# Gate weights made in the grouping stage, and scores scanned two blocks ahead at a block's end, in an eleven-stage graph network kernel

## The chip, the cores and the metric

The kernel runs on one core of a Trainium2 chip. The core has five engines with instruction streams of their own: TensorE (PE, with its weight loads as PEld), VectorE (DVE), ScalarE (ACT), GpSimd (POOL) and SyncE (SP). The metric is the device time of one execution in microseconds (us).

## The reference, cut to what matters

Four layers, each followed by a residual sum and a layer normalization over 256 columns: a rotation matrix made of 50,000 plane rotations, a relational graph attention network, a filter convolution over the edges, and a mean over the edges' sources. There are 3125 nodes and 50,000 edges sorted by destination. The change touches the second layer:

```
q_node = query[batch]                      # batch is all zeros: one query for all nodes
gh   = relu(concat([x, q_node]) @ gate_w1 + gate_b1)
gate = sigmoid(gh @ gate_w2 + gate_b2)
x0   = x * gate
h    = concat([x0, q_node, x * q_node])
h = relu(rgat(h, W1, q1, k1, b1))                  # 4 heads of 128
h = h + relu(rgat(h, W2, q2, k2, b2))              # 4 heads of 128
h = relu(rgat(h, W3, q3, k3, b3))                  # 1 head of 128

def rgat(x, W, Q, K, b):                           # 2 edge types
    xw    = einsum('ni,rio->rno', x, W)
    alpha = leaky_relu(xw[etype, dst] @ Q + xw[etype, src] @ K, 0.2)
    alpha = segment_softmax(alpha, dst)
    return segment_sum(xw[etype, src] * alpha, dst) + b
```

## The kernel before, in words

The program is a row of stages. Each has its own buffers and semaphores and ends with a barrier of all engines. The ones that matter, in order: the edge lists (`edge_order`), the grouping stage (`source_order`, buffers named bucket_), the gate stage (`nodes_gate`, gate_), then three times an attention (`attention`, sum_) and its projection (`nodes_attend`, attend_), the mixing, the filter convolution and the source mean.

Nodes stand in 25 tiles of 125. Edges are laid out in 432 steps of 125, no step crossing a node tile's border. Twelve steps are a block, so an attention has 36 blocks; a block has three parts of four steps.

The grouping stage counts the edges of each source tile and works out where each edge goes in a list by source. Nearly all of it is VectorE on arrays of 125 x 10,000; TensorE does five small products.

The gate stage takes the node tiles in seven groups of four (the last has one). Per group: `turn` multiplies by the rotation, `residual`, `statistics`, `root` (POOL), `scale` give x1; `turn_x1`, `gate_hidden`, `gate_outer`, `turn_x0` make the gate and x0; `table(t)` projects one tile on both edge types and `take(t)` adds the query's constant part and puts it in one of three output buffers (RING = 3). Before the first group it loads the gate's and projection's weights (`projection_load`), and makes the score weights (`score_weights`), the scaled weights and the query's constant rows; every engine waits for them (`ready`). SP stores a group's table rows only after x0 of the next group is made. POOL also scatters 150 edge columns (`group_edges`).

The attention's engines each run in program order:
- POOL gathers the 432 steps' rows into a ring of three blocks. A part of a slot is gathered again once the sums of the block three before it have used that part (line 1198).
- ACT scales the rows of a block by the softmax weights, 40 activations a block with four heads (`scale`), after the block's weights are made; behind a block's rows comes the exponential of the next block (`weights`).
- TensorE sums a part's four steps with `sums` into PSUM. After part 0 of block s it does `list_ends(s+1)`, after part 1 `turn_carry(s+1)`, after part 2 `turn_weights(s+1)` and `turn_scores(s+2)`.
- VectorE makes the selection matrices (`pick`), adds the sums (`add_part`), and makes the weights: `score` (needs the gathered rows of the block two ahead), `spread_in_tiles` (two scans along the edges, then `ends_made`), `spread_over_tiles`, `shift`, `grow`, `take_weights`.
- The weights of block s+1 are made while block s is summed. In block s VectorE does: load of six registers (`part_tiles`); spread_in_tiles(s+1); pick(1); add_part(0); spread_over_tiles(s+1); pick(2); add_part(1); shift(s+1); score(s+2); grow(s+1); add_part(2); take_weights(s+1); pick(s+1, 0).

Where the four steps of a part belong to one node tile, they are summed together and added once; else each is added by itself, VectorE first loads four registers (`node_tiles`), and TensorE waits for the adds. Of the 108 parts of an attention 16 are of that kind (L1466 has 120 instances in an attention, 72 + 3 x 16). VectorE's loop holds six blocks with four heads and three with one head, TensorE's and ACT's loops three.

## Time and profile before

| | us |
|---|---|
| median of 3 runs | 6628.7 (6625.0 to 6634.2) |
| the profiled execution | 6613.5 |
| its span | 6611.7 |
| gate stage, first load to the first load of the next stage | 1138 to 1586 |
| attention 1, 2, 3, first gather to last sum | 1592 to 2396, 2724 to 3530, 3763 to 4472 |

Over the span PE is busy 66%, DVE 48%, ACT 30%, POOL 54%. Times below are us from the span's start. In a row, what stands in brackets is how long the engine sat idle before the instruction and what ended that; "issue" is time in which it waited for nothing that the profile shows. Rows of a gather give POOL's time to issue it, not the transfer.

### The profile page before, as it was taken

Reading aid. Unit: us, or ns where it says so; the run is one execution under the profiler, and the core shown is the slowest. Engines: PE = TensorE matmul, PEld = TensorE weight load, DVE = VectorE, ACT = ScalarE, POOL = GpSimd, SP = SyncE. Lnnn points to the kernel's source line nnn. Section 1 sums busy time; section 2 is a strip of 40 time slices with the busy share of each in tenths; the row PEclk is TensorE's granted clock in tenths of the full one; section 3 lists DMA queues with packets and bytes.
Section 4 is the critical chain, followed back from the end, with each engine's and each line's share of the span. In section 5 each row is a group of like instructions: output and inputs, shape, how many; then the busy total and the mean of one; then the engine's idle time right before and its main releaser. Section 6 shows DMA issues by size and latency. Waiting matters only on the chain. (4 is left out here: it accounts for less than half of the span.)

```text
span 6611.7 us, 81270 instructions
## 1 busy us (share of the span) xinstructions
PE 4356.9 (66%) x17924; PEld 3140.3 (47%) x17925; DVE 3158.4 (48%) x7294; ACT 2007.4 (30%) x4713; POOL 3596.5 (54%) x2941
## 2 busy tenths in 40 slices
PE   5599720785776779676677544448788888765553
PEld 5588610443554555355556533334455555443332
DVE  6577556122554532354453244443466666433334
ACT  0122200001655520265552022211566666410000
POOL 0244410366776637776674788760355555238884
PEclk6799955797887879788786555555899999876565
DMA  0000011324665523566551233332333333233333
GB/s 7 24 10 11 10 31 42 91 62 107 168 163 138 150 72 74 127 167 157 137 151 42 46 85 84 85 77 75 80 93 94 94 94 93 67 86 84 84 84 73
DMA packets 515758, 565.41 MB, mean 86 GB/s; under 512 B 308626, under 2 KB 400639, under 8 KB 515225
## 3 DMA queue, kind: packets, MB, share of 16 engines
q0 software_dynamic: 359872, 381.65, 23.9%
q1 hardware_dynamic: 155606, 181.09, 9.7%
q14 instruction: 234, 1.92, 0.1%
q8 instruction: 46, 0.75, 0.1%
HBM read 467.37 MB, written 92.22 MB: 85 GB/s over the span
## 5 line engine op out<-in xcount | busy, mean ns | idle before, releaser
L1200 POOL DMA_INDIRECT sum_gx_sb<-scratch_xw,keep_k_row_step_sb x1296 | 1609.4, 1242 | 560.0 <-issue 361.5
L1313 PE MATMUL sum_a_ps<-sum_gx_sb,sum_sel_sb 125*125 125x258 f32 (+1 forms) x4320 | 1232.0, 450 | 554.3 <-ACT sum_gx_sb L1249 250.5
L1313 PEld LDWEIGHTS sum_a_ps<-sum_gx_sb,sum_sel_sb 125*125 125x125 f32 x4320 | 950.7, 246 | 750.6 <-issue 556.5
L1249 ACT ACTIVATE sum_gx_sb<-sum_gx_sb,sum_wt_sb 125x129 f32<-125x129 f32 x3312 | 981.7, 388 | 468.6 <-DVE sum_wt_sb L1441 468.6
L2377 POOL DMA_INDIRECT filter_gx_sb<-scratch_h,keep_k_src_step_sb x432 | 519.5, 1202 | 540.9 <-DVEq L2522 394.3
L2809 POOL DMA_INDIRECT source_gx_sb<-scratch_h,source_grouped_sb x432 | 533.6, 1235 | 155.9 <-issue 117.6
L2821 PE MATMUL source_s_ps<-source_gx_sb,source_sel_sb 125*125 125x257 f32 x864 | 376.9, 613 | 312.0 <-DMA source_gx_sb<-scratch_h,source_grouped_sb 312.0
L1107 POOL DMA_INDIRECT scratch_grouped<-keep_k_value_sb,keep_k_place_sb x400 | 476.2, 1191 | 123.7 <-issue 123.7
L2821 PEld LDWEIGHTS source_s_ps<-source_gx_sb,source_sel_sb 125*125 125x125 f32 x864 | 251.5, 305 | 437.2 <-issue 173.7
L2431 PE MATMUL filter_ps<-filter_m_sb,filter_h_sb 128*125 128x256 f32 x1760 | 407.1, 385 | 50.7 <-DVE filter_f_sb L2496 50.7
L2431 PEld LDWEIGHTS filter_ps<-filter_m_sb,filter_h_sb 128*125 128x125 f32 x1760 | 322.4, 188 | 180.5 <-issue 135.6
L2846 DVE TENSOR_TENSOR keep_agg_sb<-source_s_ps,keep_agg_sb 125x257 f32 x432 | 184.5, 427 | 391.8 <-PE source_s_ps L2821 383.7
L532 POOL TENSOR_TENSOR turn_lm_sb<-turn_lt_sb,turn_masks_sb 128x512 f32<-128x512 f32 x23 | 29.2, 1272 | 536.5 <-DVE turn_lt_sb L466 536.5
L1466 DVE TENSOR_TENSOR keep_agg_sb<-sum_a_ps,keep_agg_sb 125x516 f32 (+1 forms) x360 | 202.0, 561 | 234.8 <-PE sum_a_ps L1313 132.6
L1613 PE MATMUL attend_x_ps<-attend_w_sb,attend_ht_sb 128*125 128x512 f32 (+1 forms) x800 | 281.9, 526 | 37.3 <-ACT attend_ht_sb L2083 37.3
L2449 PE MATMUL filter_ps<-filter_ms_sb,filter_sel_sb 125*125 125x256 f32 x864 | 214.8, 392 | 135.3 <-DVEq L2521 135.3
L1242 ACT ACTIVATE sum_wexp_sb<-sum_dw_sb 48x126 f32<-48x126 f32 (+1 forms) x108 | 33.3, 308 | 719.2 <-DVEq L1431 719.2
L2492 DVE SCALAR_TENSOR_TENSOR filter_h_sb<-filter_ps,filter_lg_sb 128x1000 f32<-128x1000 f32 x111 | 133.2, 1200 | 237.8 <-issue 209.5
L2449 PEld LDWEIGHTS filter_ps<-filter_ms_sb,filter_sel_sb 125*125 125x125 f32 x864 | 153.4, 187 | 196.4 <-issue 102.5
L1448 DVE TENSOR_TENSOR sum_sel_sb<-sum_iota_sb,keep_k_dloc_sb 125x500 f32<-125x500 f32 x324 | 219.8, 678 | 45.7 <-issue 27.2
L2463 ACT ACTIVATE filter_lg_sb<-filter_lg_sb,filter_half_sb 128x1000 f32<-128x1000 f32 x220 | 238.6, 1131 | 7.6
L2421 PE MATMUL filter_ps<-filter_ea_sb,filter_m_sb 51*128 51x500 f32 x444 | 219.0, 614 | 24.8 <-DMA filter_ea_sb<-in_ea_t 24.8
(503 smaller groups left out, 7102.6 us busy)
## 6 DMA issues: line engine op xcount, KB each, us to landing
scratch_hots<-sum_cuts_sb SPq DMA_DIRECT2D x108, 244.1 KB
filter_sel_sb<-scratch_hots SPq DMA_DIRECT2D x108, 244.1 KB
sum_gx_sb<-scratch_xw,keep_k_row_step_sb POOLq DMA_INDIRECT x1296
scratch_xw<-gate_xsb_sb SPq DMA_DIRECT2D x50, 253.9 KB
scratch_xw<-attend_xsb_sb SPq DMA_DIRECT2D x50, 253.9 KB
filter_ea_sb<-in_ea_t SPq DMA_DIRECT2D x444, 24.4 KB
filter_gx_sb<-scratch_h,keep_k_src_step_sb POOLq DMA_INDIRECT x432
source_gx_sb<-scratch_h,source_grouped_sb POOLq DMA_INDIRECT x432
```

Source lines behind the costliest of these rows:

```text
L1107: nc.gpsimd.indirect_dma_start(out=dr["grouped"], out_offset=bass.IndirectOffsetOnAxis(ap=keep["place"][:, t:t + 1], axis=0), in_=keep["va ...
L1200: nc.gpsimd.indirect_dma_start(out=gx[:, q, j, :], out_offset=None, in_=table, in_offset=bass.IndirectOffsetOnAxis(ap=keep["row_step"][:, ...
L1249: last = nc.scalar.activation(here, here, ACT.Copy, scale=wt[q][:, h, j:j + 1])
L1313: last = mm(psa[b][0:P, half, 0:BF], sel[:, 0, p, j, :], gx[:, q, at, half * BF:(half + 1) * BF], **flags)
L1448: vec.tensor_tensor(sel[:, 0, p], iota[0:P, 0:P].unsqueeze(1).broadcast_to([P, HF, P]), keep["dloc"][:, bass.ds(s * T + p * HF, HF)].unsqu ...
L1613: mm(pr["psx"][r][0:P, 0:pr["width"]], x, pr["w"][:, b, r, :], start=(n == 0), stop=(n == len(blocks) - 1))
L2377: nc.gpsimd.indirect_dma_start(out=gx[:, q, j, :], out_offset=None, in_=dr["h2"], in_offset=bass.IndirectOffsetOnAxis(ap=keep["src_step"][ ...
L2431: last = mm(ps2[0:P, j, :], h1[q][:, b, j * P:j * P + P], m2[:, b, :], start=(b == 0), stop=(b == 1))
L2449: last = mm(ps3[0:P, j, :], sel[:, q, j, :], ms[:, j, :], start=True, stop=True)
L2463: nc.scalar.activation(lg[:], lg[:], ACT.Ln, scale=0.5, bias=half[0:lg.shape[0], :]).then_inc(made, 1)
L2809: nc.gpsimd.indirect_dma_start(out=gx[:, h % RING, j, :], out_offset=None, in_=dr["h3"], in_offset=bass.IndirectOffsetOnAxis(ap=grouped[:, ...
L2821: nc.tensor.matmul(pss[q % 2][0:P, j, 0:W], sel[:, q % 2, j, :], gx[:, q, j, :], start=True, stop=True).then_inc(summed, 1)
```

## The change

1. Gate weights. A new function `gate_weights` holds the projection and gate buffers in a phase around both stages. Their loads are issued at the start of the grouping stage, behind its two tables and ahead of the clearing of the grouped list. Its TensorE and VectorE streams make all that came ahead of `ready`; VectorE takes part in three places, the first behind `passed`, the second behind the large products, the third at the stage's end. In the gate stage nothing waits for `ready`; x is loaded by groups instead of whole; SP's order is new.
2. Attention. VectorE's, TensorE's and ACT's orders are new, in all three attentions.

```diff
 def source_order(...)                              # grouping stage
 sync:
+            ...loads of query, gate_b1, gate_b2, gate_w1, gate_w2, projection_load(...)
             sp.wait_ge(blanked, 1)
 tensor:
             mm(ps_step[0:1, 0:KS], ...).then_inc(listed, 1)
+            pe.wait_ge(weights_in, 16 * LOADS)
+            ...4 products gate_w1 by query; then_inc(gate_c, 1)
+            pe.wait_ge(query_rows, 1)
+            ...4 products query rows by w, 512 columns
+            score_weights(nc, pr).then_inc(scores, 1)
+            pe.wait_ge(scaled, 1)
+            ...4 products query rows by wk; then_inc(bias_made, 1)
 vector:
             dve.nop().then_inc(passed, 1)
+            dve.wait_ge(weights_in, 16 * LOADS)
+            ...query rows, 2 tensor_scalar
             ...base, running (2 large products), bucket
-            dve.drain()
+            dve.wait_ge(gate_c, 1)
+            dve.wait_ge(scores, 1)
+            ...gc, take_score_weights, 4 scalings
             vec.tensor_reduce(place[:], ...)
...
+            dve.wait_ge(bias_made, 1)
+            ...copies of xb and kb
 def nodes_gate(...), sync:
-            ...x whole, all weights; a group's table rows behind x0 of the next group
+            load_turned(0)
+            load_rows(0)
+            sp.dma_start(ident[:], dr["c_ident"]).then_inc(landed, 16)
+            load_turned(1)
+            load_rows(1)
+            next_turned(0)
+            store_x1(0)
+            next_turned(1)
+            store_x1(1)
+            store_x0(0)
+            for g in range(LAST + 1):
+                for j, t in enumerate(GROUPS[g]):
+                    store_rows(t)
+                    if j == min(1, len(GROUPS[g]) - 1):
+                        next_turned(g + 2)
+                    if j == min(2, len(GROUPS[g]) - 1):
+                        store_x1(g + 2)
+                store_x0(g + 1)
 def attention(...), scalar:
                 for j in range(T):
+                    if j == T - HF and ahead:
+                        weights(s + 1)
                     for h in range(H - 1 if j < shared * HF else H):
...
-                    scale(3 * i + q, q)
-                    weights(3 * i + q + 1)
+                    scale(3 * i + q, q, True)
 tensor, block_of, behind the sums of part p:
-                    if ahead:
-                        if p == 0:
-                            list_ends(s + 1)
-                        elif p == 1:
-                            turn_carry(s + 1)
-                        else:
-                            turn_weights(s + 1, (q + 1) % 3)
+                    if ahead and p == 0:
+                        turn_carry(s + 1)
+                    if ahead and p == 1:
+                        turn_weights(s + 1, (q + 1) % 3)
                 if ahead > 1:
                     turn_scores(s + 2)
+                    list_ends(s + 2)
 vector, block_of:
                 values = part_tiles(nc, keep, s, slice(0, 2), mybir.EngineType.DVE)
                 if ahead:
-                    spread_in_tiles(s + 1, nxt, i + (q + 1) // 3 + 1)
+                    spread_over_tiles(s + 1)
                 pick(s, q, 1)
                 add_part(s, 0, firsts, spans)
                 if ahead:
-                    spread_over_tiles(s + 1)
+                    shift(s + 1, nxt)
                 pick(s, q, 2)
+                if ahead:
+                    grow(s + 1)
                 add_part(s, 1, firsts, spans)
                 if ahead:
-                    shift(s + 1, nxt)
+                    take_weights(s + 1, nxt)
                 if ahead > 1:
                     score(s + 2, later, i + (q + 2) // 3 + 1)
-                if ahead:
-                    grow(s + 1)
                 add_part(s, 2, firsts, spans)
                 if ahead:
-                    take_weights(s + 1, nxt)
                     pick(s + 1, nxt, 0)
+                if ahead > 1:
+                    spread_in_tiles(s + 2, later, i + (q + 2) // 3 + 1)
```

Ahead of the first block TensorE now also does `list_ends(1)` and VectorE `spread_in_tiles(1, 1, 1)`.

## Rows read from the trace of the kernel before

**Rows 1.** The page's costliest groups: count, busy us, mean ns, idle and releasers.
```profile
L1200 POOL DMA_INDIRECT sum_gx_sb<-scratch_xw,keep_k_row_step_sb x1296 | 1609.4, 1242 | 560.0 <-issue 361.5
L1313 PE MATMUL sum_a_ps<-sum_gx_sb,sum_sel_sb 125*125 125x258 f32 (+1 forms) x4320 | 1232.0, 450 | 554.3 <-ACT sum_gx_sb L1249 250.5
```

**Rows 2.** Attentions 1 and 3: span, busy PE PEld DVE ACT POOL, clock, DMA, GB/s.
```profile
1592.00:2396.00 804.00, 563.62 (x2192) 423.06 (x2192) 399.70 (x1141) 448.62 (x1482) 536.28 (x433) 0.80 0.57 147
...
3763.00:4472.00 709.00, 290.23 (x1304) 237.33 (x1304) 322.76 (x1035) 142.64 (x470) 539.38 (x433) 0.51 0.33 80
```

**Rows 3.** Timeline (start, us, instruction), gate stage up to its first transpose.
```profile
1142.09 3.78 PE L1758 MATMUL gate_y_ps<-keep_mt_sb,gate_xt_sb 128*125 128x256 f32 x8 [44.46 <-DMA gate_xt_sb<-in_x_t]
...
1171.96 0.69 DVE L1895 TENSOR_TENSOR gate_xn_sb<-gate_y_ps,gate_xn_sb 125x512 f32<-125x512 f32 x1 [30.48 <-DMA gate_xn_sb<-in_x]
...
1179.87 1.05 POOL L1733 TENSOR_TENSOR gate_rsd_sb<-gate_var_sb,gate_power_sb 125x4 f32<-125x4 f32 x1 [41.81 <-DVE gate_var_sb L1905]
...
1191.22 0.48 DVE L1942 TENSOR_SCALAR gate_qb_sb<-gate_ones_sb,gate_qc_sb 128x125 f32<-128x125 f32 x2 [11.50 <-DMA gate_wt_sb<-in_W_t]
...
1192.97 20.63 PE L1597 MATMUL gate_k_ps<-gate_qk_sb,gate_wt_sb 128*128 128x8 f32 x96
...
1223.63 1.07 PE L1767 MATMUL gate_g_ps<-gate_ident_sb,gate_xn_sb 125*128 125x125 f32 x8 [1.49 <-DVEq L1960]
```

**Rows 4.** Timeline, the grouping stage's end on VectorE.
```profile
1096.33 10.57 DVE L1086 TENSOR_TENSOR bucket_running_sb<-bucket_running_sb,bucket_base_sb 125x10000 f32<-125x10000 f32 x1
...
1117.47 0.59 DVE L1090 TENSOR_SCALAR keep_k_bucket_sb<-bucket_step_ps 1x432 int32<-1x432 f32 x1
```

**Rows 5.** Who waited for whom, 1230 to 1590 (total us, times, longest).
```profile
PE gate_x_ps L1805 <- DVEq L1931: 30.5, 7, 9.0
```

**Rows 6.** Timeline, the gate stage's tables behind one such wait.
```profile
1298.11 3.65 PE L1805 MATMUL gate_x_ps<-gate_w_sb,gate_x0t_sb 128*125 128x512 f32 x4 [4.97 <-DVEq L1931]
...
1301.60 1.88 PE L1805 MATMUL gate_x_ps<-gate_w_sb,gate_x1t_sb 128*125 128x512 f32 x4
```

**Rows 7.** Timeline, attention 1, one block whose parts each lie in one tile.
```profile
2185.82 0.21 DVE L1441 COPY sum_wt_sb<-sum_c_ps 125x48 f32<-125x48 f32 x1 [0.29 <-issue]
...
2188.07 5.41 PE L1313 MATMUL sum_a_ps<-sum_gx_sb,sum_sel_sb 125*125 125x258 f32 x16 [2.75 <-ACT sum_gx_sb L1249]
2190.60 0.41 DVE L1400 TENSOR_TENSOR_SCAN sum_both_sb<-sum_mk_sb,sum_t_ps 48x125 f32<-48x125 f32 x1 [2.93 <-issue]
...
2193.59 3.75 PE L1313 MATMUL sum_a_ps<-sum_gx_sb,sum_sel_sb 125*125 125x258 f32 x16
...
2197.71 3.72 PE L1313 MATMUL sum_a_ps<-sum_gx_sb,sum_sel_sb 125*125 125x258 f32 x16
...
2201.58 0.70 DVE L1466 TENSOR_TENSOR keep_agg_sb<-sum_a_ps,keep_agg_sb 125x516 f32 x1 [0.62 <-PE sum_a_ps L1313]
...
2202.90 0.21 DVE L1441 COPY sum_wt_sb<-sum_c_ps 125x48 f32<-125x48 f32 x1 [0.62 <-issue]
...
2203.46 0.68 DVE L1448 TENSOR_TENSOR sum_sel_sb<-sum_iota_sb,keep_k_dloc_sb 125x500 f32<-125x500 f32 x1 [0.29 <-issue]
...
2205.16 1.21 PE L1313 MATMUL sum_a_ps<-sum_gx_sb,sum_sel_sb 125*125 125x258 f32 x4 [3.09 <-ACT sum_gx_sb L1249]
```

**Rows 8.** Timeline, the next block's end: its third part crosses a tile's border.
```profile
2225.05 0.21 DVE L1441 COPY sum_wt_sb<-sum_c_ps 125x48 f32<-125x48 f32 x1 [1.17 <-PE sum_c_ps L1297]
```

**Rows 9.** Line 1441 in attention 1: duration min/median/max, first and last start.
```profile
L1441 DVE COPY sum_wt_sb<-sum_c_ps x36: 206/208/209, 1636.3 to 2378.9; 125x48 f32<-125x48 f32 x36
```

**Rows 10.** Busy time by stretch, the first part's sums of Rows 7; granted clock third from last.
```profile
2188.07:2193.48 5.41, 5.41 (x19) 4.13 (x20) 2.26 (x5) 5.41 (x20) 4.50 (x4) 0.68 0.62 167
```

**Rows 11.** Timeline, attention 3, TensorE from one block to the next.
```profile
4350.53 0.37 PE L1273 MATMUL sum_t_ps<-sum_ident_sb,sum_al_sb 125*12 125x125 f32 x1
...
4352.60 2.06 PE L1313 MATMUL sum_a_ps<-sum_gx_sb,sum_sel_sb 125*125 125x129 f32 x8 [1.70 <-ACT sum_gx_sb L1249]
```

More of the change, by code:

```diff
@@ L1013, in source_order @@
         "landed", "blanked", "cleared", "counted", "totals", "spread", "begun", "passed", "listed"))
-    vec = nc.vector
+    weights_in, gate_c, scores, query_rows, scaled, bias_made = (mem.sem(n) for n in (
+        "weights_in", "gate_c", "scores", "query_rows", "scaled", "bias_made"))
+    wide_ones = mem.sb("wide_ones", [128, P])
+    vec, mm, pr = nc.vector, nc.tensor.matmul, gate["pr"]
+    LOADS = PROJECTION_LOADS + 5
     with nc.Block() as block:
@@ L1083, in _ @@
             dve.nop().then_inc(passed, 1)
+            dve.wait_ge(weights_in, 16 * LOADS)
+            for b in range(2):
+                vec.tensor_scalar(gate["qb"][:, b, :], wide_ones[:], gate["qc"][:, b:b + 1], None, ALU.mult)
+            dve.drain()
+            dve.nop().then_inc(query_rows, 1)
             vec.tensor_tensor(base[:], ps_lanes[0:P, 0:NT], base[:], ALU.add)
@@ L1090, in _ @@
             vec.tensor_scalar(keep["bucket"][:], ps_step[0:1, 0:KS], float(NT - 1), None, ALU.min)
+            dve.wait_ge(gate_c, 1)
+            dve.wait_ge(scores, 1)
+            vec.tensor_tensor(gate["gc"][:], pr["psk"][:, 128:130], gate["gb1"][:], ALU.add)
+            take_score_weights(nc, pr)
             dve.drain()
+            for b in range(2):
+                vec.tensor_scalar(pr["w"][:, 4 + b], pr["w"][:, 4 + b], gate["qc"][:, b:b + 1], None, ALU.mult)
+                vec.tensor_scalar(pr["wk"][:, 4 + b], pr["wk"][:, 4 + b], gate["qc"][:, b:b + 1], None, ALU.mult)
+            dve.drain()
+            dve.nop().then_inc(scaled, 1)
             vec.tensor_reduce(place[:], running[:].rearrange("p b t -> p t b"), AX.X, ALU.add)
@@ L1100, in _ @@
             vec.scalar_tensor_tensor(keep["place"][:], place[:], float(KS), step[:], ALU.mult, ALU.add)
+            dve.wait_ge(bias_made, 1)
+            for r in range(2):
+                vec.tensor_copy(gate["xb"][:, r, :], pr["psx"][r][0:P, :])
+            vec.tensor_copy(gate["kb"][:].rearrange("p r s -> p (r s)"), pr["psk"][0:P, 256:272])
             dve.drain()
@@ L1334, in _ @@
             turn_scores(1)
+            list_ends(1)
             def block_of(s, q, ahead):
@@ L2914, in build @@
         keep = edge_lists(keeper)
-        with phase("ends") as lists:
-            for n in ("src_tile", "dst_tile"):
-                keep[n] = lists.sb(n, [P, ET], I32)
-            with phase("order") as mem:
-                edge_order(nc, mem, dr, keep)
+        for n in ("src_tile", "dst_tile"):
+            keep[n] = keeper.sb("k_" + n, [P, ET], I32)
+        with phase("order") as mem:
+            edge_order(nc, mem, dr, keep)
+        with phase("weights") as held:
+            gate = gate_weights(held)
             with phase("bucket") as mem:
-                source_order(nc, mem, dr, keep)
-        with phase("gate") as mem:
-            nodes_gate(nc, mem, dr, keep, mt)
+                source_order(nc, mem, dr, keep, gate)
+            with phase("gate") as mem:
+                nodes_gate(nc, mem, dr, keep, mt, gate)
         agg = keeper.sb("agg", [P, NT + 1, 516])
```

129 lines of the change are left out of this document (51 added, 78 removed).

## The prediction

> **What bounds the kernel now.** I read the page's groups first, then the stretches of busy time, then the timeline of the stages that the change touches.
>
> *Attention.* The costliest group is POOL's gather: 1242 ns each and 361.5 us of issue time over 1296 of them, so 1.24 + 0.28 = 1.52 us a step when nothing else holds it, measured over undisturbed rows nearer 1.55, or about 18.6 us for a block of twelve [rows 1]. Of its 560.0 us idle, 198.5 are not issue: waits for a part of the ring to come free, that is for TensorE's sums [rows 1]. Attention 1 takes 804 us, attention 3, with one head, 709, though both gather the same 432 steps and POOL is busy the same 536 to 539 us [rows 2]. So with one head the gather paces nearly all, and with four heads the chain through TensorE, VectorE and ACT paces a large part. VectorE's take_weights (L1441) starts once a block. Its 36 starts run from 1636.3 to 2378.9, which is 742.5 us for 35 gaps, 21.2 each [rows 9]. Laid out one by one these gaps are of four kinds. Eight are at about 18.4 (the gather's pace). Ten are at 16.9 to 17.7, the chain's pace while gathered rows are in stock; one is 2202.90 - 2185.82 = 17.08 [rows 7]. Eight blocks with only their third part across a tile's border are at about 22.2, as 2225.05 - 2202.90 = 22.15 [rows 7, 8]. Nine (first or second part across, or the end of VectorE's loop) hold the rest, 742.5 - 147 - 174 - 178 = some 244.
>
> The reader should see what the 17.08 consist of: after take_weights 2.25 until the next sums start, a first part of 5.41, then 3.75 and 3.72 with gaps of 0.1 and 0.4, and from the last sum's end at 2201.43 an add, take_weights and a wait for ACT until 2205.16, that is 3.73 [rows 7]. In the first part the granted clock is 0.68 [rows 10]: it begins at the lower of the two levels (1.2 GHz) after the idle 2.75 and goes on at 2.4.
>
> *Gate stage.* From 1138 to the first transpose at 1223.63 pass 85.7 us with little computed: TensorE's second half waits for the whole of x (1171.96), VectorE for the last weights (1191.22), then come 20.63 us of score weights [rows 3]. Later TensorE is the bound, and waits seven times, 30.5 us, for `take` to free an output buffer [rows 5]; buffers come free by SP's stores, which stand behind x0 of the next group.
>
> **Part 1, grouping stage: +11.8.** TensorE gets its work when VectorE reaches `passed`, just ahead of the large product at 1096.33 [rows 4]. Step product 1.6, gate products 1.9, the query's rows by the weights 5.5 (estimates from products of that size), then score weights 20.63 [rows 3]: done near 1125.7. VectorE, with 0.6 more for the query rows, reaches its new wait at 1117.47 + 0.59 + 0.6 = 1118.7 [rows 4] and so stands still for 7.0. Behind it come the adds and four scalings, 2.4, with drains 0.4, and copies 1.5, and 0.5 for the query rows: 11.8. The new loads stand behind two tables on SP, about 35 us before they are wanted; in the gate stage the last landed by 1191.2, queued behind the whole of x [rows 3]. I hide them. Bounds: 5 (half of the wait hidden) and 30 (loads late). What is queued behind the waiting VectorE is the rest of the stage, so all of it counts.
>
> **Part 2, start of the gate stage: -65.** What is left: x turned lands 4.1 after 1138, eight products 3.78, residual 0.69, eight more 3.7 behind it, residual 0.7, then 2.5 for the statistics (second residual to POOL's root), root 1.05 with 1.6 around it, scaling and signals 1.8: about 20.5, for 85.7 before [rows 3]. TensorE waited 44.46 us for the turned x from the barrier before on [rows 3]; that part is the stage's start and unchanged. Bounds 17 and 30 (rows of x late).
>
> **Part 3, order of the stores: -43.** The seven waits go, 30.5 [rows 5], and with each the four slow products behind it, 3.65 against 1.88 [rows 6]: 7 x 1.8 = 12.4. What is late next is TensorE itself; POOL's scatter of 42.5 us a group (estimate from its instructions) stays under TensorE's 47.8. Bounds: -20 (half comes back as waits for SP) and -45. Moved past on SP are x's loads and x1's stores, each with two groups to spare. Gate and grouping together: 11.8 - 65 - 43 = -96, between -60 and -110.
>
> **Part 4, attentions with four heads: +77 each.** From the diff, one block now ends so. TensorE's last sum ends at T. VectorE adds, 0.15 + 0.70 [rows 7], picks the next block's matrices (0.45 + 0.68, and 0.6 until what follows, as the 0.62 idle in the row of take_weights), and runs spread_in_tiles(s+2): scans of 0.41 with drains and a signal, about 1.37 [rows 7]. Sum 0.85 + 1.13 + 0.6 + 1.37 = 3.95. All this time TensorE waits in list_ends(s+2), and the next block's first sums are queued behind it, although ACT has had their weights since the second part. Then come list_ends itself, 0.4, and TensorE's own register loads and branch: in attention 3, where ACT's rows are long ready, the gap from a block's last product to the next sums is 1.70 [rows 11]; 1.85 is the mean over some 33 blocks. From T to the next sums: 3.95 + 0.4 + 1.85 = 6.2, where it was 3.73.
>
> Inside the block, turn_weights now stands between the second and third part and waits for grow: +0.3 to 0.4. ACT now does the exponential ahead of the last four steps; it needs `ready(s+1)`, about 3 us after the first part. The last four steps' rows then come at ACT's pace, and the third part takes 4.4 for 3.72. The cycle: 6.2 + 5.41 + 0.35 + 3.75 + 0.7 + 4.4 = 20.8. For the first part I keep 5.41, since TensorE again stood idle before it [rows 7, 10]. Its bounds are 3.72, all at the higher level as the third part in rows 7, which gives 19.1, and 7.44, all at the lower, which gives 22.8.
>
> A cycle of 20.8 is above the gather's 18.6, so the gather paces nothing any more. The 18 plain gaps go from 8 x 18.4 + 10 x 17.4 = 321 to 18 x 20.8 = 374: +53. The eight with the third part across have half of the same additions already, in that TensorE waits for the adds one by one: 23.3 for 22.2, +9. The nine others, mostly +2 to +3 with some back at the loop's end (VectorE's loads no longer stand ahead of TensorE's wait): +15. Together +77, for two attentions +154.
>
> Here a rule of the Trainium skill speaks against my size. "Runtime: NRT & Kernel Launch", section "Instruction fetch mechanics", gives a register load about 200 ns; three would be 0.6 where the row shows 1.70 idle, and the exposed gap would be 1.1 less per block, near -77 in all. The row decides for me; the rule's case is in the first rival. For the first part, "TensorE: Matmul & The Clock Gate", section "What's actually happening", has two clock levels and the lower as the default; by it a longer idle can only make the first part slower, toward 7.44, where I stay at 5.41.
>
> **Part 5, attention 3: +15.** With one head the cycle was 14 to 15 and becomes about 16.5 (one add and one pick are shorter; the exposed 1.70 is in it already [rows 11]), under 18.6. The plain blocks stay with the gather. The 16 parts across a border eat stock that is refilled more slowly: +15, between 0 and 35.
>
> **Sum.** -96 + 154 + 15 = +73. The profiled execution takes 6613.5 and would be 6686; the median of the runs stands 15.2 above it, so 6628.7 + 73 = 6701.
>
> **Rivals.** (a) The chain grows half as much: the first sums find all rows ready and run in 3.72 instead of 5.41 [rows 7], or half of the 1.70 is hidden. Then the plain cycle is 19.1, some 26 gaps an attention are 1.7 shorter, +33 for +77, attention 3 at +5: -96 + 66 + 5 = -25, 6604. For it: ACT is ahead now. Against it: the idle before the first part is longer than the 2.75 of rows 7, and that was enough to lower the clock.
>
> (b) The scan two ahead really leaves the path: TensorE's wait in list_ends costs nothing because the next sums would wait for ACT anyway. Every plain block then goes at the gather's pace and the stock covers crossing parts; about half of POOL's 198.5 us of waits [rows 1] go. -96 - 90 = -186, 6443. For it: scans, shift and take_weights all come earlier in the block. Against it: list_ends stands ahead of the sums in TensorE's order and needs a scan that needs the last add.
>
> (c) The slower side, beyond my forecast: the first part at the lower level throughout. Point of decision: the idle before it, 6.2 for the 2.75 of rows 7. Price 2.03 more on 70 blocks: +142, 6843.
>
> (d) The gate's gain in full and the chain's growth between (a) and the forecast: 6615 to 6642, no change that could be told.
>
> (e) The change doesn't do what it says: the exponential inside the scaled rows has to wait for `ready(s+1)` and delays rows instead of hiding. That is in my sum with 0.7; if grow is late by a further 1 us, +70: 6771.
>
> **How the numbers follow.** Forecast (6650 to 6770 as its own range) 0.58, (a) 0.14, (b) 0.08, (c) 0.04, (d) 0.10, (e) 0.06. Within 0.2%, 13 us, is about what a measurement of this kernel can tell from no change. Faster: (a) less its upper edge and (b), 0.22; same: (d) and edges, 0.12; slower: forecast, (c), (e), 0.66. The range 6600 to 6780 reaches through (a) below and (e) above and leaves out (b), (c) and the far edge of (a), some 0.18.
>
> **What would show it.** In the profile after: VectorE idle about 7 us ahead of taking the score weights in the grouping stage; about 20 us from the gate stage's first load to its first transpose, and no waits of TensorE for `take`; TensorE from the last sum to the next block's first 6.2 us, that wait ended by VectorE's scan and not by ACT; gaps of take_weights near 20.8 where they were 17.1 to 18.4; the third part at 4.4; POOL's waits for TensorE up by some 150 us; attention 3 within 35 us of 709. The forecast is wrong if the first part takes 3.72 after list_ends, or if the gap from the last sum to the next stays under 4.5.

## The result, and the profile after

The changed kernel takes 6762.2 us (median, 6755.2 to 6771.3) beside 6626.9 for the kernel before: ratio 1.0206, interval 1.019 to 1.0221, or +135 us. The profiled execution of the changed kernel has a span of 6769.5 us against 6611.7, +158. It is the slowest of the four of its kernel, and the profiled one before is faster than all of its other runs, so I use the two traces for where the time went and the medians for how much.

The time by stages, each from its own first to its last row in the two traces:

| | before | changed | difference | forecast |
|---|---|---|---|---|
| grouping's end, to the gate stage's first load | 1138.0 | 1145.1 | +7.2 | +11.8 |
| from there to the first transpose | 85.7 | 19.7 | -66.0 | -65 |
| from there to the first gather of attention 1 | 368.7 | 331.9 | -36.8 | -43 |
| attention 1, first gather to last sum | 802.2 | 897.2 | +95.0 | +77 |
| attention 2 | 801.7 | 897.0 | +95.2 | +77 |
| attention 3 | 708.7 | 764.2 | +55.5 | +15 |

The first three rows sum to -95.6 (forecast -96). The attentions cost +246 (forecast +169). The other stages differ by 7.7 us in these two executions. The page's groups say the same as [rows 1], with the releasers changed:

```profile
L1256 POOL DMA_INDIRECT sum_gx_sb<-scratch_xw,keep_k_row_step_sb x1296 | 1609.3, 1242 | 796.3 <-PE sum_a_ps L1368 440.3
L1368 PE MATMUL sum_a_ps<-sum_gx_sb,sum_sel_sb 125*125 125x258 f32 (+1 forms) x4320 | 1272.1, 457 | 453.8 <-issue 233.7
```

POOL's issue is as busy as before; its idle time grew by 236 us and is now mostly waiting for TensorE. Half of TensorE's idle time before its sums is now "issue", time in which it waits for nothing that this view shows. And the wait for VectorE's scans ahead of `list_ends` (L1335), 106.5 us in the three attentions of the kernel before, is now 371.0 us, once in each of the 108 blocks:

```profile
  DVE sum_lhs_sb L1458: 371.0, 108
```

The stretches of busy time of attentions 1 and 3 (columns as in [rows 2]) show the same work in more time:

```profile
1496.70:2394.00 897.30, 583.44 (x2192) 426.65 (x2192) 401.66 (x1140) 445.40 (x1482) 540.16 (x432) 0.78 0.50 131
...
3860.40:4624.50 764.10, 289.85 (x1304) 236.59 (x1304) 319.50 (x1034) 142.63 (x470) 535.97 (x432) 0.50 0.30 74
```

A plain block of attention 1 in the timeline of the changed kernel, to be laid beside [rows 7]:

```profile
2065.58 6.31 PE L1368 MATMUL sum_a_ps<-sum_gx_sb,sum_sel_sb 125*125 125x258 f32 x16 [2.09 <-issue]
...
2072.08 3.75 PE L1368 MATMUL sum_a_ps<-sum_gx_sb,sum_sel_sb 125*125 125x258 f32 x16
...
2076.62 0.35 PE L1352 MATMUL sum_c_ps<-sum_grown_sb,sum_mk_sb 48*125 48x4 f32 x2 [0.55 <-DVE sum_grown_sb L1490]
2077.09 4.33 PE L1368 MATMUL sum_a_ps<-sum_gx_sb,sum_sel_sb 125*125 125x258 f32 x16
...
2081.56 0.69 DVE L1520 TENSOR_TENSOR keep_agg_sb<-sum_a_ps,keep_agg_sb 125x516 f32 x1 [2.87 <-PE sum_a_ps L1368]
2082.71 0.68 DVE L1502 TENSOR_TENSOR sum_sel_sb<-sum_iota_sb,keep_k_dloc_sb 125x500 f32<-125x500 f32 x1 [0.46 <-issue]
...
2084.28 0.41 DVE L1454 TENSOR_TENSOR_SCAN sum_both_sb<-sum_mk_sb,sum_t_ps 48x125 f32<-48x125 f32 x1 [0.29 <-issue]
...
2085.60 0.25 PE L1335 MATMUL sum_c_ps<-sum_hot_sb,sum_lhs_sb 48*4 48x12 f32 x4 [4.08 <-DVE sum_lhs_sb L1458]
2087.94 1.62 PE L1368 MATMUL sum_a_ps<-sum_gx_sb,sum_sel_sb 125*125 125x258 f32 x3 [2.09 <-ACT sum_gx_sb L1307]
```

Read it as a chain: the third part ends at 2081.42, then add, selection, scans, list_ends (TensorE idle 4.08), 2.09 more until the next sums, at 2087.94. The block took 22.36 us = 6.31 + 0.19 + 3.75 + 1.26 + 4.33 + 6.52. The last row names ACT, but 2.09 also stands there where the releaser is "issue" (first row): it is TensorE's own time. Over the first 35 blocks of attention 1 the medians of the six terms are 6.41, 0.19, 3.75, 1.05, 4.33, 6.54.

In what sorts of blocks did attention 1 lose? The prediction sorted its 35 gaps between starts of take_weights by their length. The 18 short ones (under 19 us before, its plain ones) went from 320.5 to 400.3 us, 22.2 each. The 17 longer ones, which it puts down to borders and loop edges, went from 422.0 to 432.8. In attention 2 it is the same: 318.0 to 402.9 and 426.3 to 427.3.

Attention 3, a block at VectorE's loop edge:

```profile
4081.92 2.05 PE L1368 MATMUL sum_a_ps<-sum_gx_sb,sum_sel_sb 125*125 125x129 f32 x8 [3.65 <-issue]
4085.84 0.23 DVE L1464 TENSOR_TENSOR_SCAN sum_state_f_sb<-keep_k_ntile_sb,sum_state_f_sb,sum_c_ps 1x12 f32 x1 [7.96 <-issue]
...
4087.95 2.05 PE L1368 MATMUL sum_a_ps<-sum_gx_sb,sum_sel_sb 125*125 125x129 f32 x8 [0.76 <-DVEq L1509]
...
4092.92 0.55 PE L1352 MATMUL sum_c_ps<-sum_grown_sb,sum_mk_sb 12*125 12x1 f32 x2 [1.27 <-DVE sum_grown_sb L1490]
...
4097.35 0.68 DVE L1513 TENSOR_TENSOR sum_cuts_sb<-sum_sel_sb,keep_k_cut_sb 125x500 f32<-125x500 f32 x1 [0.29 <-issue]
```

VectorE is idle 7.96 us for "issue", its six register loads and the loop's branch (4.4 us pass from that branch to the next instruction), before it can scan over tiles and make the second selection; TensorE's first part ended at 4083.97 and its second starts at 4087.95. The last row is an operation that only the attention with one head has: each selection is multiplied once more (`cuts`), and SP stores the product (L1276). With four heads another multiplication of 0.69 us stands in that place for the first two selections of a block (L1507).

The register loads aren't in the timeline, but they have records: the view by source line shows them (L1187, with an attention as the window). One record holds the three loads of a block on TensorE (PEldq), another the six on VectorE (DVEq); minimum, median and maximum in ns. First attention 1, then attention 3 of the changed kernel, then attention 3 of the kernel before, where the line is L1131:

```profile
L1187 DVEq TENSOR_LOAD <-keep_k_part_sb x36: 811/1147/1554, 1542.6 to 2381.5; - x36
L1187 PEldq TENSOR_LOAD <-keep_k_part_sb x36: 765/776/949, 1542.9 to 2372.9; - x36
```

```profile
L1187 DVEq TENSOR_LOAD <-keep_k_part_sb x36: 819/2519/3643, 3903.0 to 4616.7; - x36
L1187 PEldq TENSOR_LOAD <-keep_k_part_sb x36: 765/2228/2817, 3903.3 to 4613.1; - x36
```

```profile
L1131 PEldq TENSOR_LOAD <-keep_k_part_sb x36: 768/780/2294, 3803.0 to 4461.7; - x36
L1131 DVEq TENSOR_LOAD <-keep_k_part_sb x36: 811/1418/2034, 3804.4 to 4463.9; - x36
```

So in attention 3 of the changed kernel the same three loads take 2.23 us where they took 0.78 before. This is the next block's start there:

```profile
4098.20 0.26 SPq L1276 DMA_DIRECT2D scratch_hots<-sum_cuts_sb  x1
4099.25 0.25 PE L1335 MATMUL sum_c_ps<-sum_hot_sb,sum_lhs_sb 12*1 12x12 f32 x4 [3.56 <-DVE sum_lhs_sb L1458]
4103.23 2.05 PE L1368 MATMUL sum_a_ps<-sum_gx_sb,sum_sel_sb 125*125 125x129 f32 x8 [3.73 <-issue]
```

From the end of `list_ends` to the next sums pass 3.60 us (median), where it is 2.09 with four heads. The wait ahead of `list_ends` is shorter than with four heads, 3.81 for 4.27 from the last sum's end.

The gate stage, waits of TensorE between 1165 and 1491 (total us, times, longest), which answer to [rows 5]:

```profile
PE weights_x_ps L1868 <- DVEq L1978: 3.4, 3, 1.6
```

And the score weights in the grouping stage, with the wait of VectorE behind them, which answer to [rows 3, 4]:

```profile
1106.16 15.46 PE L1653 MATMUL weights_k_ps<-weights_qk_sb,weights_wt_sb 128*128 128x8 f32 x96
...
1121.73 0.16 DVE L1136 TENSOR_TENSOR weights_gc_sb<-weights_k_ps,weights_gb_sb 128x2 f32<-128x2 f32 x1 [1.86 <-PE weights_k_ps L1653]
```

### The profile page after: what moved, and what is told of

Same layout as the page of the kernel before. It is cut to its first block and busy times, and to the rows that moved or that the text cites. A ratio compares the mean times of both kernels' runs of the same rounds, so it can differ in the third digit from the quotient of the medians.

```text
span 6769.5 us, 81307 instructions
## 1 busy us (share of the span) xinstructions
PE 4379.3 (65%) x17924; PEld 3132.9 (46%) x17925; DVE 3161.7 (47%) x7294; ACT 2001.9 (30%) x4713; POOL 3598.8 (53%) x2941
## 5 line engine op out<-in xcount | busy, mean ns | idle before, releaser
L1256 POOL DMA_INDIRECT sum_gx_sb<-scratch_xw,keep_k_row_step_sb x1296 | 1609.3, 1242 | 796.3 <-PE sum_a_ps L1368 440.3
L1368 PE MATMUL sum_a_ps<-sum_gx_sb,sum_sel_sb 125*125 125x258 f32 (+1 forms) x4320 | 1272.1, 457 | 453.8 <-issue 233.7
L1335 PE MATMUL sum_c_ps<-sum_hot_sb,sum_lhs_sb 48*4 48x12 f32 (+1 forms) x432 | 26.9, 174 | 371.0 <-DVE sum_lhs_sb L1458 371.0
```

The source lines that it names most:

```text
L1256: nc.gpsimd.indirect_dma_start(out=gx[:, q, j, :], out_offset=None, in_=table, in_offset=bass.IndirectOffsetOnAxis(ap=keep["row_step"][:, ...
L1368: last = mm(psa[b][0:P, half, 0:BF], sel[:, 0, p, j, :], gx[:, q, at, half * BF:(half + 1) * BF], **flags)
```

## The experiments

Two theories to begin with. A: the parts add up, and in the attentions all that now stands between a block's last sum and `list_ends` is on the path. C: TensorE would have waited for ACT's rows or the gather anyway. Ratios are to the kernel before, run on the same chip; times of attentions are first gather to last sum in the run's trace (1, 2, 3). Where runs of different chips are compared I use ratios and stages, for the kernel before took 6618.7, 6623.9 and 6640.9 us beside them.

**gate_only**: the changed kernel with `attention` of the kernel before.

> The grouping and gate stages of the changed kernel with the attentions of the kernel before. Theory A (the two parts add up, the first gather of attention 1 came 95.6 us earlier in the changed kernel's trace): 6627 - 96 = 6531 us, and the attentions take 802, 802 and 708 us from first gather to last sum as before. Rival B (the early start is bought with transfers that still run when attention 1 begins): attention 1 longer by 10 us or more, 6541 or above.

Measured: 6523.2 us, ratio 0.9858 (0.9842 to 0.9875), attentions 804.3, 802.7, 706.6. Theory A: the gate's part is worth 95 us and costs the attentions nothing; attention 1 is 2 us longer, not 10 (rival B).

**attn_only**: the kernel before with `attention` of the changed one.

> The new attention orders alone, grouping and gate stage as before. Theory A (the parts add up): 6627 + 95 + 95 + 56 = 6873 us. Rival B (part of the loss in attention 1 comes from its earlier start after the new gate stage): attention 1 under 890 us, total under 6865.

Measured: 6868.9 us, ratio 1.0372 (1.0354 to 1.0389), attentions 895.2, 897.1, 762.6. Attention 1 isn't under 890, so rival B is out here too. The two parts add up in the stages: -95.6 and +245.7 in the table. In the medians they are -95 and +250, which is 155 beside the 135 of the two kernels' runs, taken on another chip; the 20 us between them stay open.

**pick_first**: the pick ahead of the last add.

```diff
+                if ahead:
+                    pick(s + 1, nxt, 0)
                 add_part(s, 2, firsts, spans)
-                if ahead:
-                    pick(s + 1, nxt, 0)
```

> The changed kernel, with the next block's first selection matrices made ahead of the last part's add instead of between the add and the scans. Theory A (everything between the last sum and list_ends is on the path, for TensorE's next sums are queued behind that wait): the gap from the last sum to the next first sum falls by the pick, from 6.5 to about 4.8 us with four heads and from 7.7 to about 5.5 with one; 1.7 x 60 blocks + some 45 with one head (then the gather's 18.6 us a block is the floor) = -150, 6612 us. Rival C (the next first sums would have waited for ACT's rows anyway): the gap stays above 6, 6750 to 6762 us.

Measured: 6638.9 us, ratio 1.0031 (1.002 to 1.0042), attentions 853.4, 862.2, 719.7. In attention 1 the gap from last sum to next sum fell from 6.54 to 5.23 (median), with one head from 7.75 to 6.02. Moving this one step took 123 us off the three attentions (44, 35 and 45), for 150 expected; the ratio fell by 1.75%. That speaks against theory C: most of what was moved was on the path. With one head the time came as expected (45) though the gap fell by 1.7 and not by 2.2.

**scan_early**: nothing between last sum and `list_ends`.

```diff
 vector:
                 pick(s, q, 2)
+                if ahead > 1:
+                    score(s + 2, ...)
                 if ahead:
                     grow(s + 1)
                 add_part(s, 1, firsts, spans)
                 take_weights(s + 1, nxt)
-                score(s + 2, ...)
+                spread_in_tiles(s + 2, ...)
+                pick(s + 1, nxt, 0)
                 add_part(s, 2, firsts, spans)
-                pick(s + 1, nxt, 0)
-                spread_in_tiles(s + 2, ...)
 tensor:
                         turn_weights(s + 1, (q + 1) % 3)
+                        turn_scores(s + 2)
-                    turn_scores(s + 2)
                     list_ends(s + 2)
```

> The changed kernel with scores two ahead made ahead of the second part's add, turned between second and third part, and scanned ahead of the last part's add; the pick too ahead of the last add. Nothing of VectorE then stands between the last sum and list_ends. Theory A: gap from last sum to next first sum 2.3 to 3 us, cycle 17 to 18.5, so the gather (18.6 a block) is the bound of the plain blocks; attention 1 about 770 us (before 802, changed 897), attention 3 about 690, total 6440 to 6490 us. Rival C: gap above 5, no faster than 6700. Rival D (scores two ahead so early stand waiting for the gather, and hold back VectorE): gap short, but the wait comes back between second and third part; 6530 to 6650 us.

Measured: 6563.9 us, ratio 0.992 (0.9904 to 0.9937), attentions 807.4, 815.9, 726.6. The gap is gone (median 1.29 us) and with it 90 and 81 us of the 95 lost. But the plain blocks are no faster than in the kernel before; what was gained at the end came back inside. Part of it came as rival D has it: the gap between second and third part rose from 1.05 to 1.94 (median, attention 1), and `score` now waits for gathered rows, in attention 1 as follows (us in total, times, longest), where it was 3.6 us in the changed kernel and 20.7 in the kernel before:

```profile
DVE sum_sc_sb L1447 <- DMA sum_gx_sb<-scratch_xw,keep_k_row_step_sb: 33.7, 19, 4.8
```

The gap between first and second part rose more, from 0.19 to 2.05. A block at VectorE's loop edge in this run's timeline:

```profile
1646.80 0.70 DVE L1521 TENSOR_TENSOR keep_agg_sb<-sum_a_ps,keep_agg_sb 125x516 f32 x1 [0.76 <-PE sum_a_ps L1368]
1647.60 3.72 PE L1368 MATMUL sum_a_ps<-sum_gx_sb,sum_sel_sb 125*125 125x258 f32 x16 [0.93 <-DVE keep_agg_sb L1521]
1654.16 0.23 DVE L1465 TENSOR_TENSOR_SCAN sum_state_f_sb<-keep_k_ntile_sb,sum_state_f_sb,sum_c_ps 4x12 f32 x1 [6.66 <-issue]
...
1656.87 5.82 PE L1368 MATMUL sum_a_ps<-sum_gx_sb,sum_sel_sb 125*125 125x258 f32 x16 [1.09 <-DVEq L1510]
```

VectorE sits 6.66 us on register loads and the loop's branch, and TensorE, done with the first part at 1651.32, waits until 1656.87 for the second selection behind them. That wait was none of the rivals I had; it became theory I. The time, 6563.9, lies in rival D's range, and no run tells what each of the two waits costs.

**early2**: scan_early with VectorE's loads moved behind `pick(1)` and `spread_over_tiles`, and TensorE's loads ahead of `list_ends`.

```diff
-                values = part_tiles(..., mybir.EngineType.DVE)
-                if ahead: spread_over_tiles(s + 1)
                 pick(s, q, 1)
+                if ahead: spread_over_tiles(s + 1)
+                values = part_tiles(..., mybir.EngineType.DVE)
```

> As scan_early, and the register loads out of the way: VectorE loads its six behind the second selection and the scans over tiles (in scan_early they stood ahead of them, 3.4 us, and 6.7 at its loop's edge, where TensorE waited between first and second part), TensorE its three ahead of list_ends. Theory A: gap between first and second part under 1 us in plain blocks, the gather the bound of plain blocks; attention 1 770 to 790 us, attention 3 700 or less: 6490 to 6515 us. Rival H (the loads only move their idle: the first part's add is late, and the third part waits for it): no faster than 6550 us.

Measured: 6598.3 us, ratio 0.996 (0.9946 to 0.9974), slower than scan_early; attentions 809.9, 822.7, 759.5. In attention 1 the gap from first to second part fell (median 2.05 to 0.66 us), and the gap from second to third rose from 1.94 to 3.96. With one head the latter went from 3.97 to 7.31. Rival H: moving the loads along VectorE's stream only moves the idle.

**regs_ahead**: the changed kernel, TensorE's loads ahead of its wait.

```diff
                 if ahead > 1:
                     turn_scores(s + 2)
+                    spans = spans_of(s + 1) if q < 2 else None
                     list_ends(s + 2)
```

> The changed kernel; TensorE loads the next block's three registers ahead of its wait for the scans instead of behind it, in two blocks of three (the third stands at its loop's edge). Theory A (loads and branch are the 1.7 to 1.85 us between list_ends and the first sums, and exposed): gap from last sum to next first sum 6.5 to about 5.0 in those blocks, -1.5 x 24 x 2 = -72, and about as much per block with one head (-25): 6660 to 6670 us. Rival F (a register load costs about 0.2 us, what the Trainium skill states, and the rest is the branch): -0.6 x 24 x 3 = -43, 6720 us.

Measured: 6680.9 us, ratio 1.0085 (1.0068 to 1.0102), attentions 853.4, 855.1, 768.5. `list_ends` and the next sums in its trace:

```profile
2047.38 0.25 PE L1335 MATMUL sum_c_ps<-sum_hot_sb,sum_lhs_sb 48*4 48x12 f32 x4 [4.08 <-DVE sum_lhs_sb L1463]
2047.90 5.78 PE L1368 MATMUL sum_a_ps<-sum_gx_sb,sum_sel_sb 125*125 125x258 f32 x16 [0.27 <-issue]
```

0.27 us for 2.09: the loads with the register instructions that belong to them were all of it and cost 1.8 us a block, 43 us an attention for 24 blocks, against rival F. The record of the loads themselves is 0.78 us of that. With one head the gap at the block's end fell too (7.75 to 4.58) but the one behind the first part grew from 1.16 to 4.14, and attention 3 gained nothing. So there VectorE, not TensorE, sets the pace. VectorE's loads still take 2.52 us (median) in this run's attention 3.

**turn6**: the changed kernel with `turn = 6` for one head too.

> The changed kernel with VectorE's loop of six blocks for one head too, instead of three, so that half of its 11 loop edges go (one edge every six blocks). Theory I (with one head VectorE's own stream is the bound: its six register loads stand behind the scans and ahead of the second selection, and at a loop's edge TensorE waits 4.0 us between first and second part instead of 0.4 to 1.5): attention 3 falls from 764 by 6 x 3 = 18 us to about 746, the four-head attentions stay at 897; 6744 us. Rival J (TensorE's chain is the bound, the edges are covered): attention 3 stays above 758, 6755 to 6770 us.

Measured: 6743.5 us, ratio 1.0156 (1.0132 to 1.0181), attentions 894.3, 894.0, 742.3. Attention 3 fell by 22 us, six edges fewer at 3.7 each: theory I. In the trace of the changed kernel 4.4 to 5.5 us pass from VectorE's branch at such an edge to its next instruction.

**exp_behind**: the changed kernel with ACT's exponential behind a block's rows.

> The changed kernel with the exponential again behind a block's scaled rows instead of ahead of its last four steps. Theory A (ACT stands waiting for the shifted scores with its last four steps undone, so that TensorE's third part runs at ACT's pace, 4.33 for 3.72): third part 3.72 to 3.8 us, the gap ahead of it unchanged at 1.0; -0.6 x 60 = -36, 6720 to 6730 us. Rival G (ACT is not ahead of TensorE by then, and the exponential comes later): the gap ahead of the third part grows by 2 us or more, 6850 us or above.

Measured: 6728.3 us, ratio 1.0167 (1.0148 to 1.0187), attentions 883.0, 873.8, 763.2. In attention 1 the third part is 3.72 for 4.33 (median), the gap ahead of it 1.12 for 1.05. As theory A has it: the exponential inside the rows is a cost of 0.6 us a block, 14 and 23 us an attention with four heads.

**warm**: six products of constants ahead of `list_ends`, results overwritten.

```diff
                     turn_scores(s + 2)
+                    for n in range(3):
+                        for half in range(banks):
+                            mm(psa[0][...], ident[0:P, 0:P], keep["dloc"][:, 0:BF], start=True, stop=True)
                     list_ends(s + 2)
```

> The changed kernel; TensorE, ahead of its wait for the scans at a block's end, does products of constants into sum buffer 0 (free by then) whose result is overwritten: the same wait, but busy for about 3 us of it. Theory A (the first part takes 6.4 us instead of 3.7 because TensorE begins it at the lower clock after idling): first part 3.7 to 4.5 us with four heads, granted clock of an attention up, cycle 20.5 or less; -2 x 50 to 70 = -100 to -140, 6620 to 6660 us. Rival E (the first part is paced by something else, ACT's rows or the weight loads): first part stays at 6 or more, 6750 to 6775 us.

Measured: 6726.5 us, ratio 1.015 (1.0133 to 1.0167), attentions 867.0, 876.0, 763.0. Granted clock in attention 1 0.78 to 0.85:

```profile
1499.10:2366.10 867.00, 655.42 (x2600) 487.61 (x2600) 401.60 (x1140) 445.43 (x1482) 538.44 (x432) 0.85 0.52 136
```

The first part's mean fell from 6.50 to 5.55 us in attention 1, some 33 us, and the attentions with four heads by 30 and 21. It fell to 3.72 in some blocks only. Another:

```profile
2084.15 2.77 PE L1408 MATMUL sum_a_ps<-keep_k_dloc_sb,sum_ident_sb 125*125 125x258 f32 x12
2088.60 0.24 PE L1335 MATMUL sum_c_ps<-sum_hot_sb,sum_lhs_sb 48*4 48x12 f32 x4 [1.68 <-DVE sum_lhs_sb L1461]
2091.58 5.50 PE L1368 MATMUL sum_a_ps<-sum_gx_sb,sum_sel_sb 125*125 125x258 f32 x12 [2.73 <-issue]
```

TensorE does its products, and is still idle 1.68 and 2.73 us before the sums, which start slowly again. Theory A in kind, some 40% of it in size (-51 us in the two attentions for -120); how much more clock there is to win was not separated.

**gate_warm**: the same products in gate_only, at a block's end, four heads only.

> As gate_only; TensorE, in the attentions with four heads, does products of constants at each block's end, while it would wait for ACT's first rows. Theory A (the first part begins at the lower clock after idling, 5.4 to 6.7 us in most blocks; in the blocks that the chain paces that time is on the path): first part 3.7 to 4 us in most blocks, clock of an attention above 0.85, attentions 10 to 30 us shorter each: 6465 to 6505 us. Rival E (the saved time comes back as a wait for ACT's rows or the gather, which pace the first part's end): first part shorter but the gap behind it longer; 6515 to 6535 us.

Measured: 6549.7 us, ratio 0.9864 (0.9839 to 0.9888), attentions 808.7, 808.8, 709.0; gate_only had ratio 0.9858. The granted clock rose from 0.81 to 0.86, the first part's median fell from 5.41 to 3.72, and nothing was won. One block of its timeline:

```profile
2099.81 3.72 PE L1369 MATMUL sum_a_ps<-sum_gx_sb,sum_sel_sb 125*125 125x258 f32 x16
2103.99 0.24 PE L1336 MATMUL sum_c_ps<-sum_hot_sb,sum_lhs_sb 48*4 48x12 f32 x4 [0.46 <-DVE sum_lhs_sb L1464]
2105.58 3.72 PE L1369 MATMUL sum_a_ps<-sum_gx_sb,sum_sel_sb 125*125 125x258 f32 x16 [1.35 <-DVEq L1515]
```

The first part ends at 2103.53 and the second starts at 2105.58, behind VectorE's scans and selection. So rival E holds here: the first part is shorter and the gap behind it longer (0.72 to 1.91, median of attention 1). In the order of before the lower clock in the first part was covered by VectorE. In the changed order it is not: there the gap behind the first part is 0.2 us.

**stores_old**: gate_only with SP's whole order of the gate stage as before: table stores again behind x0 of the next group, and with them x's later loads and x1's stores in their old places.

> As gate_only (6523 us), but SP stores a group's table rows again only behind x0 of the next group, loads by groups and early weights kept. Theory A (the seven waits of TensorE for `take`, 30.5 us, come from this order): TensorE waits again about seven times, 25 to 31 us, and the stretch from the first transpose to the first gather grows from 326 to 360; 6523 + 27 to 40 = 6550 to 6563 us. Rival K (the waits came from the queue being behind the whole load of x, or from the lower clock behind the waits only): under 10 us more, below 6535 us.

Measured: 6581.4 us, ratio 0.9912 (0.9889 to 0.9936), first gather at 1534.8 for 1490.4, +44. Theory A, slightly larger than expected; TensorE's seven waits are back:

```profile
PE weights_x_ps L1864 <- DVEq L1974: 32.9, 7, 9.2
```

One more wait is back with them, 7.4 us for a tile of x1, which gate_only doesn't have. It came with the rest of the order, and belongs to the +44.

**gate_long_loops**: gate_only with VectorE's loops of 12 and 6 blocks.

```diff
-    turn = 6 if H == 4 else 3
+    turn = 12 if H == 4 else 6
```

> As gate_only, with VectorE's loops of twelve blocks with four heads (before six) and six with one head (before three), so that half of its loop edges go. Theory I (an edge costs VectorE 3 to 4 us more than another block's start, and the block there loses that): three edges an attention with four heads less, -5 to -9 each, six with one head, -6 to -18: 6490 to 6510 us. Rival L (edges are covered by the gather's stock): 6515 to 6530 us.

Measured: 6496.2 us, ratio 0.9781 (0.9757 to 0.9804), attentions 786.7, 788.3, 710.7. Three edges fewer are worth 14 to 18 us an attention with four heads, more than twice the middle of what I expected, and with one head, where the gather paces the order of before, nothing. The stages give -28 against gate_only, the ratios -0.8% (some 50); why they differ stays open, the chip of the second was slower by 22 us over the kernel before. It is the fastest of all, and beats both kernels.

## Why the prediction was right, and where its steps were off

The forecast was 6701 for 6762 us, slower, inside the range. The direction was right because the step at the block's end was; the size was not: +73 was forecast and +135 measured. The gain came out right by a balance of two errors, which is luck; the loss was too small in two places.

*What bounds now.* The kinds of gaps stood the test (18 short ones as I had them; of the others seven at 21 to 23.5 and ten longer, where I had eight and nine), but one reading was wrong. I took the 17.08 of [rows 7] as a chain through TensorE with 5.41 of first part in it. In gate_warm that part took 3.72 and the same block still took 17.14: the first part's length did not set the pace there, and the row behind it names VectorE. It cost me nothing in the sum, since the changed order does expose the first part.

*Part 1, +11.8, measured +7.2.* The mis-sized term is the score weights, 20.63 from [rows 3]. There TensorE ran them behind an idle stretch at a granted clock of 0.50, the lower level throughout. In the grouping stage it had just done 7.7 us of products, ran them at 0.68 and took 15.46, so VectorE waited 1.86 and not 7.0. The stretches of busy time of the two, the kernel before and the changed one (granted clock third from last):

```profile
1192.97:1213.60 20.63, 20.63 (x97) 20.53 (x97) 0.16 (x1) 0.00 (x0) 0.00 (x0) 0.50 0.00 1
```

```profile
1106.16:1121.62 15.46, 15.46 (x97) 15.36 (x95) 13.63 (x3) 0.00 (x0) 0.00 (x0) 0.68 0.00 1
```

So the duration of a row was carried to a place with another clock.

*Part 2, -65, measured -66.0.* Right: from first load to first transpose 19.7 for 20.5. The terms one by one were not compared.

*Part 3, -43, measured -36.8.* Mechanism right, shown by stores_old (its seven waits are those of [rows 5]). Three waits of 3.4 us together stay; the other 3 us aren't traced.

*Part 4, +77, measured +95.* The step that carries the case, "the next block's first sums are queued behind" `list_ends`, was right, shown by pick_first and scan_early. Its terms, forecast and measured median: end of block 6.2 and 6.54; first part 5.41 and 6.41; gap to the third 0.7 and 1.05; third part 4.4 and 4.33. The first part is the mis-sized term. I kept a row in which TensorE had been idle for 2.75; now it is idle 4.08 and again 2.09, and in this block the granted clock is 0.58 for 0.68 in [rows 10]. I had named 7.44 as the upper bound and gone by the lower row. The rule of the Trainium skill that I set beside it ("TensorE: Matmul & The Clock Gate", "What's actually happening") pointed the right way. By sorts of blocks there is a second balance: the plain gaps lost 80 us for 53, the others 11 for 24. POOL's waits for TensorE grew by 242 us in all (440.3 for 198.5), for some 150 forecast.

The register loads: the gap of 1.70 [rows 11] held with four heads, 1.8 us by regs_ahead. By the other rule cited from the Trainium skill ("Runtime: NRT & Kernel Launch", "Instruction fetch mechanics", 200 ns a register) three loads would be 0.6, an estimate. The trace has 0.78 for the three with four heads, near the rule; the other 1.0 us are the register instructions behind them, which the rule doesn't speak of and which the path pays as well.

*Part 5, +15, measured +55.5.* Here the step failed in kind: "the plain blocks stay with the gather". The cycle was forecast at 16.5, under the gather's 18.6; it was 20.7 (median), its mean 20.3 for 18.8 before. Three terms were off or missing. First, "the exposed 1.70 is in it already": the gap from `list_ends` to the sums is 3.60 in the new place, because the three loads take 2.23 and not 0.78. That, and not the selection, is why a block's end takes 7.75; the selection is cheaper with one head, as I had it. Second, I did not count VectorE's own six loads, whose record grew from 1.42 to 2.52 (medians; 39 us over the attention). With them it is idle 3.9 to 5.5 us, and 7.5 to 9.0 at a loop edge, whose branch went from 2.9 to 4.5 us (medians of the ten edges). With four heads such stretches lie under a first part of 6 us; with one head the first part is 2.06. Third, the gap while turn_weights waits is 2.97 ahead of the third part, for 1.42 before. regs_ahead and turn6 show that VectorE's stream is what bounds it.

Why the loads are slower can be read from the traces, though no run took the cause away. In the changed kernel 35 of TensorE's 36 load records of attention 3 begin 1.1 to 1.6 us behind SP's issue of a store of `cuts`, and take 1.65 to 2.8 us; the one that begins later takes 0.77. Of VectorE's 36, the 25 that begin 0.8 to 1.0 us behind it take 2.2 to 3.6 us, and the 11 that begin more than 5 us behind it 0.8 to 1.5. In the kernel before, TensorE's begin 3.1 us or more behind such a store, and 34 of the 36 take under 1. In pick_first, where the selection and its store come earlier, the median is 1.41, and VectorE's 1.56; in early2, where VectorE's begin 0.65 us (median) behind a store, it is 2.97. With four heads there is no such store, and no load of TensorE is over 1.2 us, although the DMA engines are busier there (0.50 for 0.30) and the two engines load at the same distance from each other (first starts 1542.6 and 1542.9, 3903.0 and 3903.3 in the rows above). So the new order seems to have laid the loads of two engines into the shadow of a store; how the store holds them up is open.

*The rivals.* (a) is out: the sums found their rows ready, but took 6.41 and not 3.72, and nothing of the 1.70 was hidden; with it (d), which stood between (a) and the forecast. (b) is out: scans two ahead did not leave the path in the order given; in scan_early, where they do, the attentions still only return to before's time, since waits for gathered rows, the crossing parts and VectorE's loads hold it. (c), the lower clock throughout, was half true: 1.0 of its 2.03 us. (e), the exponential, costs its 0.6 and no more.

## What to carry to other kernels

Moving work off one engine's wait helps only if no engine that stands on the path has to wait for it in program order: before placing a step at the end of a block, list what is queued behind its consumer. Carry a duration to another place only with the clock that its engine will have there, and ask first whether a slow stretch is on the path at all (here a shorter first part gave back 20 to 30 us an attention in one order, nothing in the other). Count register loads and loop edges as instructions of their engine: in the timeline they are only "issue", but the view of their own line has their durations. And look at those durations in the place where a step will stand, not only where it stood: the same loads took three times as long there.

## What the runs showed of the hardware

- Three register loads on TensorE took 0.78 us (median) in the attentions with four heads, and with the register instructions behind them 1.8 us of the path. Six on VectorE took 1.15 us and left it idle for 2.4 to 3.7 us inside a loop's body and 6.5 to 7.9 at its edge.
- The same three loads took 2.23 us (median) and the six 2.52 in attention 3 of the changed kernel, where all but one of TensorE's and 25 of VectorE's 36 begin within 1.6 us of SP's issue of a store of 125x500 numbers; in the kernel before, where TensorE's begin 3.1 us or more behind it, they took 0.78 and 1.42.
- From VectorE's branch at a loop's edge to its next instruction pass 3.5 to 5.5 us in the changed kernel. Doubling VectorE's loop bodies took 14 to 18 us off an attention with four heads for three edges less, so 5 to 6 us an edge (an estimate from these times).
- The same 96 score-weight products took 20.63 us at a granted clock of 0.50 and 15.46 at 0.68.
- Filling TensorE's idle time with products raised the granted clock of an attention from 0.78 to 0.85; it shortened the attention only where nothing else ended later.
